# Moving mask, reciprocal and weight preparation off GpSimd in a paged-attention kernel

## The reference, cut to what matters

```python
x1 = einsum('bct,bcd->bdt', x, w0[cond])              # level 0, one 32x32 matrix per batch row
q, k, v = x1 @ Wq, x1 @ Wk, x1 @ Wv                   # level 1, 8 query heads, 4 key groups, width 32
q, k = rope(rms(q)), rope(rms(k))
k_blocks[blk, :, off] = k; v_blocks[blk, :, off] = v  # paged cache, blocks of 16 positions
scores = q . k_all * SCALE
allowed = (kpos <= pos) & (kpos > pos - 128)
p = softmax(where(allowed, scores, -inf))
o = (p @ v_all) @ Wo
y = o @ W_base + lora(o, adapter)                     # level 2
out = y + einsum('bct,bcd->bdt', y, w3[subject])      # level 3, one 32x32 matrix per batch row
```

## Time and profile before

| | us |
|---|---|
| median of three runs | 305.37 (302.78 to 307.06) |
| the profiled execution | 302.65 |
| its span from first to last instruction | 300.8 |
| preparation, up to GpSimd's first use of the lists | 59.3 |
| stage 1, up to the landing of the last scatter | 70.4 |
| from there to the first value matmul | 19.7 |
| value matmuls of tiles 0 to 15 | 139.0 |
| rest | 12.5 |

### The profile page before, as it was taken

The page is one execution under the profiler, slowest core; times in us unless marked ns, Lnnn a source line. Parts: engine busy times, 40 slices in busy tenths (PEclk is TensorE's granted clock), DMA queues, the critical chain, the costliest instruction groups (busy, mean ns, idle before and its releaser), DMA issues.

```text
span 300.8 us, 7985 instructions
## 1 busy us (share of the span) xinstructions
PE 210.8 (70%) x2402; PEld 155.9 (52%) x2402; DVE 209.0 (69%) x628; ACT 131.8 (44%) x491; POOL 164.2 (55%) x279
## 2 busy tenths in 40 slices
PE   0132599699899993005788876897868879988773
PEld 0112475455555551004667755675657667767641
DVE  0987947888699985204589876784884867878760
ACT  0220015155444553321756664465555744667510
POOL 4456856067555557754266666556656665673120
PEclk9999859799999998555799998997997998999998
DMA  5819995034611000023031434233424343331011
GB/s 151 258 34 209 211 381 112 17 107 136 194 55 46 29 20 35 32 64 97 4 111 55 118 89 129 73 110 93 142 58 113 95 128 74 115 104 58 20 37 35
DMA packets 18319, 29.70 MB, mean 99 GB/s; under 512 B 8189, under 2 KB 13640, under 8 KB 17906
## 3 DMA queue, kind: packets, MB, share of 16 engines
q0 software_dynamic: 7408, 19.04, 22.9%
q1 hardware_dynamic: 8130, 5.22, 6.0%
q10 hardware_dynamic: 2752, 5.08, 5.4%
HBM read 29.43 MB, written 7.34 MB: 122 GB/s over the span
## 4 chain that ended last, share of the span: by engine, by line
issue 28%; POOL 24%; PE 19%; DMA 16%; DVE 4%; POOLq 4%; ACT 3%; SPq 0%; ACTq 0%; DVEq 0%
DMA big<-in_pool,row_now 4%; DMA w0c<-in_w,w_i 4%; PE quad L1119 4%; POOL own L547 4%; PE quad L1171 4%; POOL big L482 3%; POOL work L504 3%; PE bank L1157 3%; POOL big L542 3%; DMA merged<-work,row_now 2%; POOLq L422 2%; POOL merged L517 2%; DMA big<-merged,row_now 2%; POOL w0c L436 2%; DMA con<-in_consts 2%
## 5 line engine op out<-in xcount | busy, mean ns | idle before, releaser
L699 ACT ACTIVATE work<-bank,nmx 128x164 f32<-128x164 f32 x128 | 49.6, 398 | 30.3 <-DVE nmx L981 24.7
L1157 PE MATMUL bank<-kt_rope,big 128*128 128x164 f32 x256 | 46.8, 319 | 0.0
L1157 PEld LDWEIGHTS bank<-kt_rope,big 128*128 128x128 f32 x256 | 43.4, 205 | 5.0 <-issue 0.8
L995 DVE TENSOR_TENSOR onT<-quad,rT 32x256 f32<-32x256 f32 x64 | 26.9, 420 | 21.9 <-PE quad L1171 20.4
L1153 PE MATMUL bank<-mask,identb 128*128 128x492 bf16 (+1 forms) x48 | 18.2, 379 | 30.3 <-DVE kt_rope L972 22.7
L981 DVE TENSOR_REDUCE nmx<-bank 128x3 f32<-128x492 f32 (+1 forms) x48 | 28.5, 593 | 12.3 <-PE bank L1157 12.1
L1119 PE MATMUL quad<-wqkv_sb,work 128*128 128x512 f32 x64 | 34.2, 660 | 2.8 <-ACT work L652 2.7
L988 DVE STREAM_TRANSPOSE work<-work 128x768 f32<-128x768 f32 (+2 forms) x96 | 34.7, 410 | 0.0
L682 ACT ACTIVATE big<-qT,con 128x256 f32<-128x256 f32 (+1 forms) x64 | 27.2, 512 | 0.1
L517 POOL DMA_INDIRECT merged<-work,row_now x16 | 18.3, 1141 | 15.4 <-ACT work L646 9.0
L436 POOL DMA_INDIRECT w0c<-in_w,w_i x16 | 16.9, 1054 | 17.9 <-DMA w0c<-in_w,w_i 7.1
(11 more groups left out here) (158 smaller groups left out, 469.6 us busy)
## 6 DMA issues: line engine op xcount, KB each, us to landing
merged<-big ACTq DMA_DIRECT2D x3, 1024.0 KB
xin<-in_x SPq DMA_DIRECT2D x16, 128.0 KB
out<-x4s SPq DMA_DIRECT2D x16, 128.0 KB, 2.0
w3bd<-in_w SPq DMA_DIRECT2D x64, 4.0 KB
con<-in_consts SPq DMA_DIRECT2D x1, 660.5 KB, 5.2
wqkv_sb<-in_wqkv ACTq DMA_DIRECT2D x1, 512.0 KB
wt_sb<-in_wt ACTq DMA_DIRECT2D x1, 256.0 KB
wp_sb<-in_wp ACTq DMA_DIRECT2D x1, 256.0 KB
```

Source lines behind the costliest of these rows:

```text
L699: act.activation(prob[:, p, hd, 0:NK], ps_sc[(p + i) % 2][:, j * NK:j * NK + NK], ACT.Exp, bias=nmx[:, p, hd:hd + 1], scale=1.0, accum_out ...
L995: ve.tensor_tensor(onT[rows, :, :].rearrange("p c (b n) -> p b c n", b=NB), ps_o[rows, :, 64 * (g % 2):64 * (g % 2) + 64].rearrange("p b ( ...
L1157: mm = pe.matmul(at[:, j * NK:j * NK + NK], qbd[:, p, hd, :], kT[:, p, hd // GSZ, 0:NK], start=False, stop=(j == n - 1), skip_group_check= ...
```

## The change

Four things change.

1. The mask of all 16 tiles is built in two VectorE instructions before the first `keys`, as 1 where masked and 0 elsewhere; `identb` becomes -1e30 times the identity, so that identity times mask gives what it gave before. TensorE indexes the mask by tile.
2. The reciprocals are written by VectorE straight into the 256 columns of `rwide`, with the 8 sums read through a broadcast. `rden` and GpSimd's spreading are gone.
3. w3 plus identity is built once (load, one VectorE addition over 32 partitions x 256, store to a DRAM scratch). The diagonals are loaded from there and used by TensorE as they are; `w3i` is gone, and a refill of `w3bd` waits for `l3_done`.
4. GpSimd's stage 2 is unrolled, the gathers use `idx` columns without copies (in `cached` in stage 1 too), and only `zm`, `fetch` and `cached` are left in a step.

```diff
-        mask = sb("mask", [128, 2, NK], BF16)
+        mask = sb("mask", [128, NT, NK], BF16)
...
@@ sync
+            sp.dma_start(w3e[:, :, :], w3.rearrange("n c d -> c n d")).then_inc(s_w3e, 16)
             def phase1(h, u):
...
             sp.wait_ge(s_zero, ZEROED)
+            sp.wait_ge(w3e_done, 1)
+            sp.dma_start(w3_d.rearrange("n c d -> c n d"), w3e[:, :, :]).then_inc(s_w3d, 16)
+            sp.wait_ge(s_w3d, 16)
...
                     if reused(t):
-                        sp.wait_ge(w3i_done, t - 1)
-                    diagonal(t, p, w3, subj_sb, w3bd, s_w3)
+                        sp.wait_ge(l3_done, t - 1)
+                    diagonal(t, p, w3_d, subj_sb, w3bd, s_w3)
@@ gpsimd
             def cached(t, r):
-                pl.tensor_copy(row_now[:, 0, r:r + 1], idx[:, 0, bass.ds(t, 1)]).then_inc(row4_copied, 1)
-                wait(row4_copied, t + 1)
                 pl.indirect_dma_start(
                     out=kvb[:, r, :], out_offset=None, in_=pool_rows4,
-                    in_offset=bass.IndirectOffsetOnAxis(ap=row_now[:, 0, r:r + 1], axis=0),
+                    in_offset=bass.IndirectOffsetOnAxis(ap=idx[:, 0, t:t + 1], axis=0),
...
-            def masks(t, p):
...
-                if isinstance(h, int) and NT <= 4 * h + u < NT + 2:
-                    masks(4 * h + u - NT, u % 2)
...
             def fetch(t, r, n):
-                pl.tensor_copy(row_now[:, 1:3, r:r + 1], idx[:, 1:3, bass.ds(t, 1)]).then_inc(rowm_copied, 1)
-                wait(rowm_copied, t + 1)
                 wait(s_cache[r], 16 * (n + 1))
...
-            def phase2(h, u):
-                t, k, p, r, n = at_step4(h, u, 1)
-                if valid(t):
-                    wait(rden_done, t + 1)
...
-                    for c in range(2):
-                        pl.tensor_copy(rwide[...], rden[...]).then_inc(rwide_done, 1)
+            for s in range(NT + 2):
+                t = s - 2
                 if valid(t):
                     wait(zs_done, t + 1)
...
-                    wait(s_w3[p], 64 * (k + 1))
-                    if reused(t):
-                        wait(l3_done, t - 1)
-                    pl.tensor_tensor(w3i[:, p, :], w3bd[:, p, :], ident, ALU.add).then_inc(w3i_done, 1)
-                t, k, p, r, n = at_step4(h, u, -1)
-                if valid(t) and reused(t):
-                    wait(sc_done, 3 * (t - 1))
-                    masks(t, p)
...
+                t = s + 2
+                if valid(t):
+                    fetch(t, t % RING, t // RING)
+                t = s + 3
+                if valid(t) and t >= RING:
                     wait(pv_done, t - 3)
-                    cached(t, r)
+                    cached(t, t % RING)
@@ scalar
-            act.copy(identb[:, :], ident).then_inc(s_prec, 1)
+            act.activation(identb[:, :], ident, ACT.Copy, scale=NEG).then_inc(s_prec, 1)
@@ vector, before same_blocks
+            ve.wait_ge(s_w3e, 16)
+            ve.tensor_tensor(w3e[:, :, :], w3e[:, :, :], cc("ident", TOK)[:, 0:TOK].unsqueeze(1)
+                             .broadcast_to([TOK, 8, TOK]), ALU.add).then_inc(w3e_done, 1)
@@ vector, before keys(0, 0, 0, 0)
+            for k, (name, a, b, op) in enumerate((("backpos", 0, NKB, ALU.is_lt), ("ownpos", NKB, NK, ALU.is_gt))):
+                ve.tensor_tensor(mask[:, :, a:b], cc(name).unsqueeze(1).broadcast_to([128, NT, b - a]),
+                                 pos3[:, k, :].unsqueeze(2).broadcast_to([128, NT, b - a]), op).then_inc(mask_done, 1)
@@ vector, phase2
                     ve.wait_ge(exp_done, H * (t1 + 1))
-                    ve.reciprocal(rden[:, p1, :], den[:, p1, :]).then_inc(rden_done, 1)
+                    if not isinstance(t1, int) or t1 >= 1:
+                        ve.wait_ge(rT_done, t1)
+                    ve.reciprocal(rwide[:, :].rearrange("p (c g d) -> p c g d", c=GSZ, g=G),
+                                  den[:, p1, :].rearrange("p (g c) -> p c g", c=GSZ).unsqueeze(3)
+                                  .broadcast_to([128, GSZ, G, HD])).then_inc(rwide_done, 1)
@@ tensor
-                    pe.wait_ge(mask_done, 2 * (t + 1))
+                    pe.wait_ge(mask_done, 2)
...
-                          mask[:, p, :].unsqueeze(1).broadcast_to([128, n, NK]), start=True, stop=False,
+                          mask[:, bass.ds(t, 1), :].broadcast_to([128, n, NK]), start=True, stop=False,
...
-                    pe.wait_ge(w3i_done, t3 + 1)
-                    pe.matmul(ps_l3, w3i[:, 1 - p, :], x3s[:, 1 - p, :], start=True, stop=True).then_inc(l3_done, 1)
+                    pe.wait_ge(s_w3[1 - p], 64 * (k3 + 1))
+                    pe.matmul(ps_l3, w3bd[:, 1 - p, :], x3s[:, 1 - p, :], start=True, stop=True).then_inc(l3_done, 1)
...
-                    pe.wait_ge(rwide_done, 2 * (t1 + 1))
+                    pe.wait_ge(rwide_done, t1 + 1)
```

More of the change, by code:

```diff
@@ L124, in build @@
     merged = nc.dram_tensor("merged", [SEGS * BLOCK, ROW], F32).ap()
+    w3_d = nc.dram_tensor("w3_scratch", [8, TOK, TOK], F32).ap()
     blocks_d = nc.dram_tensor("blocks_scratch", [B, SPAN], F32).ap()
@@ L168, in build @@
         w3bd = sb("w3bd", [128, 2, 128])
-        w3i = sb("w3i", [128, 2, 128])
+        w3e = sb("w3e", [TOK, 8, TOK])
         qsc = sb("qsc", [128, HD])
@@ L346, in build @@
         on_used = sem("on_used")
-        s_blank, w3i_done = sem("s_blank"), sem("w3i_done")
-        pT_done, pv_done, rden_done = sem("pT_done"), sem("pv_done"), sem("rden_done")
+        s_blank = sem("s_blank")
+        s_w3e, w3e_done, s_w3d = sem("s_w3e"), sem("w3e_done"), sem("s_w3d")
+        pT_done, pv_done = sem("pT_done"), sem("pv_done")
         rwide_done = sem("rwide_done")
@@ L554, in _ @@
             fetch(1, 1, 0)
-            def phase2(h, u):
-                t, k, p, r, n = at_step4(h, u, 1)
-                if valid(t):
-                    wait(rden_done, t + 1)
-                    if not isinstance(t, int) or t >= 1:
-                        wait(rT_done, t)
-                    for c in range(2):
-                        pl.tensor_copy(rwide[:, 128 * c:128 * c + 128].rearrange("p (g d) -> p g d", g=G),
-                                       rden[:, p, :].rearrange("p (g c) -> p c g", c=2)[:, c].unsqueeze(2)
-                                       .broadcast_to([128, G, HD])).then_inc(rwide_done, 1)
-                t, k, p, r, n = at_step4(h, u, 2)
+            for s in range(NT + 2):
+                t = s - 2
                 if valid(t):
                     wait(zs_done, t + 1)
-                    if not isinstance(t, int) or t >= 1:
+                    if t >= 1:
                         wait(l2_done, t)
@@ L572, in phase2 @@
                                      zs[:, :].rearrange("p (b c) -> p b c", b=NB),
-                                     zscale[:, bass.ds(t * NB, NB)].unsqueeze(2).broadcast_to([E * R, NB, TOK]),
+                                     zscale[:, t * NB:t * NB + NB].unsqueeze(2).broadcast_to([E * R, NB, TOK]),
                                      ALU.mult).then_inc(zm_done, 1)
-                    wait(s_w3[p], 64 * (k + 1))
-                    if reused(t):
-                        wait(l3_done, t - 1)
-                    pl.tensor_tensor(w3i[:, p, :], w3bd[:, p, :], ident, ALU.add).then_inc(w3i_done, 1)
-                t, k, p, r, n = at_step4(h, u, -1)
-                if valid(t) and reused(t):
-                    wait(sc_done, 3 * (t - 1))
-                    masks(t, p)
-                t, k, p, r, n = at_step4(h, u, -2)
+                t = s + 2
                 if valid(t):
-                    fetch(t, r, n)
-                t, k, p, r, n = at_step4(h, u, -3)
-                if valid(t) and (not isinstance(t, int) or t >= RING):
+                    fetch(t, t % RING, t // RING)
+                t = s + 3
+                if valid(t) and t >= RING:
                     wait(pv_done, t - 3)
-                    cached(t, r)
-            steps(pl, phase2, NT + 2, *P2R[1:])
+                    cached(t, t % RING)
         @block.scalar
```

21 lines of the change are left out of this document (6 added, 15 removed).

## The result

The changed kernel took 322.37 us in the median of four runs (320.80 to 323.42); the kernel before had 304.11 us beside it. The ratio is 1.058 with an interval of [1.053, 1.063]: 5.8% slower. The profiled execution took 323.42 us, with a span of 321.2 us where the kernel before had 300.8: 20.4 us more. Three executions of the later runs took 682.74 and 1074.94 us (the changed kernel, second session) and 680.97 us (the last variant, fifth session); no trace of them was kept and nothing explains them, the medians count them and the ratios don't.

A forecast was written before the change was run, and what follows sets the result against it. GpSimd bounded stage 2, with VectorE close behind and to become the bound. 302.65 us profiled + 11.0 for stage 2 - 4.5 for the rest = 309.2; with the median 2.7 above, 312 us, 2.2% slower, range 289 to 319.

The forecast's parts named there:

- that gap follows the value matmuls, which shift with it: VectorE's turn in stage 2: its only idle gap, 0.46 us, cannot hide the wide reciprocal; turn 7.93 to 9.93 us.
- overlay, own rows: The two parts of `fetch` in GpSimd's stage 2 loop, behind the gather's landing: 1.11 and 1.00 us.
- The reciprocal: VectorE, stage 2: widening from 8 to 256 columns costs 2.16 us against 0.16, 2.0 us more per step.
- ends: Reciprocals of tiles 0 and 15, outside the fourteen turns: 2.0 us each, less some 0.5 of TensorE lateness, together 3.0.
- rest -4.5: Mostly stage 1: masks off GpSimd -3.4, gathers without index copies -1.0, first two `fetch` -0.5, w3 addition +0.4.
- half price: Rival: reciprocal at 5 ns a column, 1.4 us, turn 9.2; 300 us, no change within 2%; chance 0.09.
- the forecast's case: Wide reciprocal on VectorE at 8 ns a column, 6.3 to 9.0; 306 to 317 us, chance 0.68.
- VectorE becomes the bound, GpSimd's floor is 8.9 us: Stage 2: VectorE's turn grows to 9.93 us, above GpSimd's loop of gather, landing and `fetch` at 8.9 us.
- streams one column a cycle: Rival: cheap wide reciprocal on VectorE, turn 8.2, GpSimd's 8.9 us step sets the pace; 290 us, chance 0.19.
- the masks' cover: VectorE's 10.51 us idle before the first keys hides building all masks, about 2.9 us.
- the index copies of stage 1: GpSimd, stage 1: without them four gathers start some 0.25 us earlier each, -1.0, and the first two `fetch` -0.5.
- SyncE's queue: Wait on `l3_done` behind diagonal loads and an output store: 6.2 us within a step of 9.9, hidden, priced at nothing.

The follow-up runs named there:

- the last variant: Changed kernel with 8-column reciprocal spread by VectorE, `fetch` behind cache gather and value matmuls, masks behind the last scatter's descriptors: 288.26 us, ratio 0.943.
- The run with the late `fetch`: Changed kernel, wide reciprocal kept, GpSimd's `fetch` waiting for the value matmuls: 300.70 us on chip 1, 301.04 us on chip 10.
- chip 10: Chip of the first two sessions; the changed kernel repeated there unchanged took 301.89 us, ratio 0.994 to the kernel before.
- the narrow one: Reciprocal of 8 columns instead of 256 in the changed kernel: 286.11 us when VectorE spreads it, 285.95 us when GpSimd does.
- chip 1: Chip of the fourth session; the changed kernel repeated there unchanged took 323.12 us, ratio 1.061 to the kernel before, with gaps.

## Why the prediction was right or wrong

**The step that failed** is "that gap follows the value matmuls, which shift with it". The forecast moved the value matmuls and left their length at 1.4 us. They grew by 1.6 us in twelve tiles, 12 x 1.6 = 19 us, and two stretches at the lower clock added 2 x 1.4 us more. The run with the late `fetch` shows this on one chip: 22.4 us. The reading of the row was wrong too: the 0.46 us gap of the earlier trace rows stands before `nmx` and ends with the scores (`bank`, L1157), not with the value matmuls. The cause lies one line further on in the order of GpSimd, which the prediction listed ("overlay, own rows") and did not place in time: once GpSimd has nothing else to do, `fetch` is released by `zs`, and `zs` stands right in front of the transposes that release the value matmuls. In the kernel before the longer list of GpSimd's work kept `fetch` away from them in nearly every tile.

**The reciprocal** was the right mechanism with a wrong size: 1709 ns instead of 2160, (1709 - 161) / 248 = 6.2 ns per column past the eighth, just below the 6.3 to 9.0 ns of the prediction. The slope from the 12-column row was too steep; the 8-column row with the fixed part taken off had it. The reading of the Trainium skill, "VectorE: DVE Perf Modes", section "Walkthrough: the 8-slice pipeline in each mode", as 8 cycles a column gave 2.13 us; the measurement is below it, and far above one column a cycle. Put in, it gives a turn of 7.93 + 1.55 = 9.48 (9.30 measured on chip 10), fourteen turns of 132.7, +1.7 for the 130.98 of the earlier trace rows, ends some +2.1 (2 x 1.55 less the 1.0 that the prediction took off), rest -4.5: 302.0 us for 302.65 before, on the scale of the profiled execution. The changed kernel has 300.9 to 301.9 on the three chips without the gaps. With the 19.2 and 2.8 us above it would be 324.0, where the first profiled execution took 323.42. So the two errors went against each other, and that the kernel came out slower, as forecast, was luck: without the gaps there is no change within 2%, which is what the rival *half price* said and the forecast's case did not.

**VectorE becomes the bound, GpSimd's floor is 8.9 us:** right. With the wide reciprocal VectorE is without a pause but for 0.46 us in its turn on chip 10; with the narrow one the loop of gather, landing and `fetch` comes out at 8.73 us. Its rival "streams one column a cycle" forecast 290 us for a kernel with no reciprocal to pay, and 286 to 288 was measured. The two large parts of the change thus cancel: GpSimd's relief brings the time to 0.942 of what it was, 17 us less, and the wide reciprocal takes back 301.89 - 286.11 = 15.8 us (both on chip 10).

**The rest, -4.5:** only -1.6 arrived at the first keys. At VectorE's first turn it is -2.4, but that isn't this term alone: the wide reciprocal of tile 0 is in it with +1.5, and a wait of 1.26 us for `quad`, which the gaps of tile 0 made in the trace of before, is gone. The masks took 2.92 us in the idle time, as forecast (2.9), and the last GpSimd product of stage 1 came 2.8 us earlier (120.01 for 122.84). But the masks' cover was taken for free: they held GpSimd's row copy for 1.6 us on the way to the first `fetch`. What the index copies of stage 1 were worth (-1.0 and -0.5 in the forecast) no run separates. Part of the difference between executions is the clock: in the first trace TensorE ran at its 1.2 GHz level from 56 to 62 us and a group of four projections took 3.78 us; on chip 10 the clock was full there and the same group took 1.98 us, and the first keys came at 133.09.

**SyncE's queue** was priced at nothing, which holds: ScalarE's waits in the trace after name `nmx` and the level-3 products, not an output store.

**What stays open.** What TensorE lacks in the gaps, and why sessions differ. The trace shows only that nothing it records ends them, that the clock is full, that the three gaps stand at nearly the same places in each tile (behind the 41st to 44th matmul, and twice between the 81st and the 94th), and that the 16 KB instruction transfers are not beside all of them: tiles 7 to 10 have the gaps without one, and on chip 10 one lies inside the whole group of tile 2. Chip and hour aren't separated, since the gaps were seen in two sessions, and only chip 10, without the large gaps, was used twice. The chip of the first measurement isn't known; that it is of chip 1's kind is an inference from equal times and equal gaps.

## What to carry to other kernels

When an engine is relieved, ask not only which engine is next, but at what moment its remaining DMAs will now be issued, and what runs then. Before one experiment is read against a measurement of another session, repeat the unchanged kernel beside it: here a wait in stage 1 that is worth next to nothing looked like 22 us. A long VectorE instruction placed in VectorE's idle time is not free if GpSimd is on the path at that moment.

## What the runs showed of the hardware that was not expected

- One program, two times by session: 322.4 and 323.1 us in two sessions, 301.9, 300.9 and 300.9 us in three others, on three other chips than chip 1, while the kernel before stayed within 1.3 us. The difference is gaps of 0.2 to 0.7 us in TensorE's issue of short matmuls (32 rows, 96 in 1.38 us) while GpSimd issues indirect DMAs. A small form of it shows on chip 10 too: an overlay issued 0.74 us behind the first value matmul stretches the 96 starts to 1.80 us.
- A VectorE instruction with two inputs in SBUF holds GpSimd: a copy of 0.19 us took 1.81 us (123.21 to 125.02), until the first mask instruction (122.72, 2.25 us long) was just done, and an indirect DMA of 0.99 us took 2.41. The Trainium skill, "SBUF — State Buffer", section "SBUF: two separate sides", says that the two engines share a port pair that one of them holds for a whole instruction; the trace agrees for the copy, which ends 0.05 us behind the first mask instruction.
- A reciprocal costs 6.2 ns per column of 128 partitions in float32, some six times a product's 0.97 ns, and a broadcast input doesn't save it: 8 values read out to 256 columns took 1.71 us where the 8 alone took 0.16.
